# Twelve filler matmuls at the end of each half-layer segment, taken out

## What is computed

```
def _ln(x, scale, bias):
    m = jnp.mean(x, axis=-1, keepdims=True)
    v = jnp.var(x, axis=-1, keepdims=True)
    return (x - m) * jax.lax.rsqrt(v + EPS_LN) * scale + bias

for i in range(NUM_BLOCKS):                      # 8
    residual = x
    Q = fmap(x @ Wq[i] + bq[i])                  # fmap = elu + 1
    K = fmap(x @ Wk[i] + bk[i])
    value = x @ Wv[i] + bv[i]
    KV = jnp.einsum('nsh,nsh->nh', K, value)
    Ksum = jnp.sum(K, axis=1)
    Z = 1.0 / (Q * Ksum[:, None, :] + EPS_ATTN)
    V = Q * KV[:, None, :] * Z
    attn_out = gelu(V @ Wo[i] + bo[i])
    x = _ln(attn_out + residual, ln1_s[i], ln1_b[i])
    residual = x
    h = gelu(x @ W1[i] + b1[i])                  # 128 -> 512
    ff_out = gelu(h @ W2[i] + b2[i])             # 512 -> 128
    x = _ln(ff_out + residual, ln2_s[i], ln2_b[i])
```

## Time and profile before

| | us |
|---|---|
| median of 3 executions | 760.48 |
| lowest, highest | 756.5, 760.8 |
| the profiled execution, its own time | 754.89 |
| its span, first to last instruction | 753.0 |
| mean granted TensorE clock of it | 0.929 |

### The profile page before, as it was taken

How to read it: one execution, slowest core, us unless ns; L and a number is a source line. 1 busy time by engine, 2 the same in 40 slices (tenths; PEclk the granted TensorE clock), 3 DMA queues, 4 the chain that set the end, 5 groups by cost and what they waited for, 6 DMA issues and landing times.

```text
span 753.0 us, 9757 instructions
## 1 busy us (share of the span) xinstructions
PE 676.7 (90%) x3427; PEld 456.7 (61%) x3427; DVE 440.8 (59%) x1036; ACT 315.5 (42%) x501; POOL 113.4 (15%) x93
## 2 busy tenths in 40 slices
PE   9976999899996699999999999999859998899996
PEld 5656577688773355555555555555547875565595
DVE  5579332545767466666666666666645577353344
ACT  3054103354423455555555555555515541244341
POOL 0120130033100011111111111111141271000000
PEclk9599879999998799999999999999978996699997
DMA  3011667000030001010000101010000000000000
GB/s 82 27 46 44 181 177 160 1 1 0 1 126 14 0 1 42 1 43 2 28 14 13 29 3 39 0 42 0 1 0 1 0 1 1 0 1 0 1 0 29
DMA packets 43498, 21.74 MB, mean 29 GB/s; under 512 B 14399, under 2 KB 40571, under 8 KB 43464
## 3 DMA queue, kind: packets, MB, share of 16 engines
q1 hardware_dynamic: 43464, 21.28, 10.5%
HBM read 20.68 MB, written 0.52 MB: 28 GB/s over the span
## 4 chain that ended last, share of the span: by engine, by line
PE 49%; issue 29%; DVE 14%; POOL 5%; ACT 2%; POOLq 0%; DVEq 0%
PE ps L1408 8%; PE ps L1423 8%; POOL rstd L488 5%; PE ps L1626 5%; PE ps L1198 4%; PE ps L1642 4%; PE ps L1648 2%; PE ps L1191 2%; PE ps L1244 2%; PE ps L1338 1%; DVE z L987 1%; PE ps L1365 1%; PE ps L1505 1%; PE ps L1325 1%; PE ps L1517 1%
## 5 line engine op out<-in xcount | busy, mean ns | idle before, releaser
L1198 PE MATMUL ps<-filler 128*128 128x512 bf16 x380 | 101.0, 409 | 1.5 <-POOL filler L476 0.9
L488 POOL TENSOR_TENSOR rstd<-rv,minus_half 128x4 f32<-128x4 f32 x34 | 46.8, 1377 | 345.8 <-DVE rv L817 345.8
L997 DVE SCALAR_TENSOR_TENSOR zr<-ps,zr 128x512 fp32r<-128x512 f32 x96 | 65.1, 690 | 53.5 <-ACT zr L652 53.2
L652 ACT ACTIVATE zr<-ps 128x512 fp32r<-128x512 f32 x96 | 57.4, 598 | 68.0 <-PE ps L1408 63.8
L1517 PE MATMUL ps<-wl,z 128*128 128x128 f32 x512 | 67.9, 282 | 5.4 <-ACT z L707 5.4
L1505 PE MATMUL ps<-cf,wl 128*128 128x512 f32 x128 | 62.7, 612 | 7.0 <-ACT cf L564 7.0
L1517 PEld LDWEIGHTS ps<-wl,z 128*128 128x128 f32 x512 | 60.7, 192 | 12.0 <-ACT z L707 8.2
L1155 DVE SCALAR_TENSOR_TENSOR z<-z,kc 128x512 f32<-128x512 f32 x48 | 34.7, 751 | 49.3 <-ACT z L767 49.3
L1198 PEld LDWEIGHTS ps<-filler 128*128 128x128 bf16 x380 | 38.8, 104 | 40.5 <-issue 9.9
L1408 PE MATMUL ps<-zr 128*128 128x512 f32 x192 | 61.8, 404 | 0.9 <-DVE zr L973 0.9
L1423 PE MATMUL ps<-zr 128*128 128x512 f32 x192 | 59.4, 391 | 2.0 <-DVE zr L997 2.0
(11 more groups left out here) (253 smaller groups left out, 1163.3 us busy)
## 6 DMA issues: line engine op xcount, KB each, us to landing
wl<-in_L_attn_W SPq DMA_DIRECT2D x16, 256.0 KB
big<-in_L_cond_weight SPq DMA_DIRECT2D x32, 64.0 KB, 1.8
arena<-in_L_cond_expert_wi SPq DMA_DIRECT2D x1, 1024.0 KB, 9.2
arena<-in_L_cond_expert_wo SPq DMA_DIRECT2D x4, 256.0 KB, 6.4
big<-in_L_ffn_q_w SPq DMA_DIRECT2D x2, 512.0 KB
big<-in_L_ffn_k_w SPq DMA_DIRECT2D x2, 512.0 KB
tree_v<-in_L_ffn_v_w SPq DMA_DIRECT2D x2, 512.0 KB
arena<-in_L_cond_share_wi SPq DMA_DIRECT2D x1, 768.0 KB, 5.4
```

Of the source, the lines that this page charges most:

```text
L488: nc.gpsimd.tensor_tensor(rstd[:, half, :], rv[:, half, :], minus_half[:, :], ALU.pow).then_inc(S_["rstd"], 1)
L652: nc.scalar.activation(hidden_part(h, n, 0), ps[h][:, n % 2, :], ACT.Relu).then_inc(S_[k + "_hi"], 1)
L997: V.scalar_tensor_tensor(hidden_part(h, n, 1), ps[h][:, n % 2, :], 0.0, hidden_part(h, n, 0), ALU.max, ALU.subtract).then_inc(S_[k + "_lo" ...
L1198: T.matmul(bank, filler[:, :].to_broadcast([P, P]), filler[:, :].to_broadcast([P, HT]), start=True, stop=True)
```

## The change

The call `keep_warm(12, ps[b][:, 0, :])` at the end of PE's segment is removed. Nothing else is touched: no wait, no buffer, and no other engine's program.

```
@@ -1551,8 +1551,6 @@
                 if m is not None:
                     ffn_out(m, b, sb_, (2, 3))

-                    keep_warm(12, ps[b][:, 0, :])
-
             def layer(l, s, next_loaded):
                 segment(l, 1, s, l, 0, s)
                 arrived(1 - s, next_loaded)
```

## The result

The kernel without the twelve fillers took 771.46 us (median; 769.85 to 772.34) against 758.66 for the kernel before in the same comparison: the ratio is 1.0166, with a 95% interval of 1.0124 to 1.0209. It is slower by about 13 us. The profiled execution took 772.34 us, with a span of 770.5 us and a mean granted clock of 0.896 (0.929 before). Three slow executions, one of `e8_early` (3565 us), one of the kernel before (3210 us) and one of `e9_early_gates` (757.83 us), are left out of the ratios in this document.

The account below looks back on a forecast made before the run. In the layers PE was taken as the bound outside a hole ended by DVE's `xn`. Direct term 0 plus 15 falls of 1.0 us gave 15 us, put on a 760.48 us median: 775 us, range 765 to 788.

Parts of the forecast that it names:

- The fillers are off the path: Segment end: PE waits for `xn` until 406.10 either way, so removing 2.78 us of fillers gives 0 directly.
- The clock falls in nearly every hole: Before each first turn: 2.83 us idle loses the clock in nearly all 15 holes, or within some 3 us behind.
- one row of before showed 2.70 us survived: PE idle from 237.4 to 240.1 us: clock still 1.00 at 240.1, lost at 242.8 after a second, shorter idle piece.
- the row with 1.40 us idle and thin work around it: Ahead of the first expert stage, small work around the idle: clock fell to 0.50 from 137.0 to 140.4 us.
- 1.0 us for each fall: Turn and L1505 behind each hole: a 3.4 us stretch at half clock loses about 1.0 us, between 0.45 and 1.7.
- the sum: All layers: 15 falls of 1.0 us each give 15 us, with bounds 7 and 26.
- 0.45 us for a slow turn: Start of turn to start of L1505: 1.98 us at the low clock instead of 1.53.
- about twice: Streaming at clock 0.50: fp32 matmuls of 512 columns take 0.82 us each against 0.47.
- a value between two placements: Low stretch beginning inside the hole costs 0.45 us, beginning with L1505 1.7; 1.0 was taken between these ends.
- The sentence that set this aside: In pricing a fall: a longer segment moves the next hole against the clock's ups and downs, not summable from rows.
- The long low stretch: Rival: behind each hole the clock stays low 6 us or more, 2.7 us lost each, 40 in all, 800; chance 0.07.
- The fall at a few holes only: Rival: a third to a half of the 15 holes lose the clock, 5 to 7 us, 766; chance 0.06.

Follow-up runs that it names:

- e8_early: Kernel before, its twelve fillers kept, with 4 more fillers at the start behind the small matmuls L1228 to L1236: ratio 0.9895.
- e9_early_gates: Kernel before with 4 early fillers, and 4 + 2 fillers ahead of the gate matmuls of both expert stages: ratio 0.9935.
- e10_six: Kernel before with six fillers instead of twelve at each segment's end: 768.23 us, ratio 1.0138.
- e6_after_pad: Changed kernel (no fillers at segment ends) with an extra ACT copy before each attention gelu: 773.48 us, ratio 1.0178 to the kernel before.
- e4_alternate: Kernel before with the twelve fillers kept only at every other segment (8 of the 15): 768.52 us, ratio 1.0129.
- e12_both: Kernel before with 4 early fillers, one behind each of six L1244-stage token tiles, and 4 + 2 ahead of both stages' gate matmuls: 748.73 us, ratio 0.9885.

## Why the prediction was right

Forecast 775 us, 765 to 788, slower. Measured 771.46. By its steps:

- *The fillers are off the path; their removal gives nothing back.* Right. Eight of them do as well as twelve (1.0009), and the turn's wait for `xn` ends at the same distance from `attn_out` with and without them (6.41 and 6.42 us).
- *The clock falls in nearly every hole.* Right, 15 of 15, although one row of before showed 2.70 us survived. The choice to go by the row with 1.40 us idle and thin work around it was borne out: the runs place the change between 1.10 us idle (held), 1.53 (some) and 1.97 (all). The advice of the Trainium skill ("TensorE: Matmul & The Clock Gate", section "Why this matters for your kernels"), by which a gap of this length would have kept the clock, does not agree with these runs: a third less idle time lost it at every hole.
- *1.0 us for each fall.* Measured 0.94 in the settled segments, and 13.1 us for the layers where the sum had 15: 14 periods between the first and last `attn_out` carry the price, and the fifteenth fall, at 562 us, replaces part of the longer low stretch that the kernel before has at the layers' end. The size was near, and in part by luck. The sum had 0.45 us for a slow turn and the rest for part of L1505; in the settled segments the low stretch begins 0.6 us behind the turn's start, the turn is not slow (0.66 us), and L1505 pays it all. (A piece of L1505 wholly at the low clock takes 3.69 us against 1.98, 1.9 times as long, while the rows that I gave for "about twice" come to 1.7.) That the place of the low stretch sets the price was right, and the runs bear it out: a low stretch of 3.4 us costs 1.4 us where it begins 1.5 us behind the turn's start (`e10_six`), 0.94 at 0.6 us behind it (the changed kernel), and 20.48 - 19.75 = 0.73 at 0.2 us ahead of it (`e6_after_pad`). But I took a value between two placements, as if each hole had its own. The experiments show that the low stretches settle at 20.48 us apart, and the loss is 20.48 - 19.54. The sentence that set this aside, that a longer segment moves the next hole and that I could not sum it, named the term that decides. With every second hole closed, an open one costs 1.91 (`e4_alternate`), so the estimate would have failed there.
- *The rivals.* The long low stretch came at one hole, the fifteenth, behind which the code has no pairs of fillers. It was near for the others: without the pairs of fillers it comes at every third, and with every second hole closed at each open one. The fall at a few holes only is what six fillers give. Neither was the case of the change as a whole.
- *What would be seen.* PEclk 0.91 in the layers, period 20.5, idle 2.84 before the turn, the other engines unchanged: all as written. PE's busy time fell by 676.7 - 656.4 = 20.3 us, the 42 us of fillers less some 20 of slower matmuls.
- *The median.* I put the sum on 760.48, and the comparison with the changed kernel has the kernel before at 758.66: 1.8 us. Fourteen times 0.94 for fifteen times 1.0 is another 1.8. Together they are about the 3.5 us between forecast and measurement.

What stays open: what decides whether a hole of 1.5 us loses the clock, beyond that it varies from hole to hole; what keeps the low stretches 20.48 us apart; and why the low stretch in `e4_alternate` lasts 6.8 us where the changed kernel's lasts 3.4. It fits that there it begins before the turn (the row from 410.00 is low, the turn is at 411.33), so that the idle time and the thin work fill it, but no run took this apart. In `e6_after_pad` it begins before the turn too, by 0.2 us only, and lasts 3.4 us.

## What to carry to other kernels

Filler matmuls cost nothing where they fit in a hole of TensorE that another engine ends, and they can hold the clock for the dense work behind it. Before they are taken out, look in the granted clock for stretches of the same kernel with as much idle time or as thin work, and price one fall by how much dense work on the path follows within the low stretch. Try the number of fillers: here eight was as good as twelve, and four no better than none. In a periodic loop don't add the prices of single falls: the loop can settle on the spacing of the low stretches, and then a small saving or addition can change nothing in a settled segment: four fillers and an added copy of 0.20 us both left it at 20.48 us.

## What the hardware showed that I had not expected

- Twelve matmuls of one row each (2.79 us of busy PE, no idle) lost the clock like an empty hole; twelve of 128 rows, as long, held it.
- The loop settled at 20.48 us per segment, with none and with four fillers, and with 0.20 us of work added; in the changed kernel 3.4 us at half speed and then 17 at full, 14 times in a row.
- Open holes at every second segment made each low stretch twice as long, 6.8 us, and each open hole twice as dear, 1.91 us instead of 0.94; the layers took as long with every second hole open (307.9 us) as with all of them (307.3).
- A fall avoided in one stage (17.5 to 38 us) was followed by a new one in another (51.4 us, and 50.5 in `e12_both`), which had none in the other twelve traces.
